# One core, sixteen attention bodies: TensorE's projections and scores moved ahead of the global queries' turn, and four of twelve key transfers handed to GpSimd

## What is computed

```python
def _layernorm(x, axis=-1, eps=1e-05): ...
mask = local(block of 64) | is_global[:, None] | is_global[None, :]   # 8 global tokens
q = split_heads(x @ Wq + bq)          # 16 heads of 8
k = split_heads(x @ Wk + bk)
v = split_heads(x @ Wv + bv)
scores = jnp.einsum('bhqd,bhkd->bhqk', q, k) / scale
scores = jnp.where(mask[None, None], scores, -jnp.inf)
attn = jax.nn.softmax(scores, axis=-1)
out = jnp.einsum('bhqk,bhkd->bhqd', attn, v)
return out.transpose(0, 2, 1, 3).reshape(B, S, E) @ Wo + bo
x = x + _L0_attn_ref(_layernorm(x, axis=-1), ...)
```

## Time and profile before

| | us |
|---|---|
| median of 3 runs | 567.05 (566.04 to 572.32) |
| profiled execution, its own time | 568.54 |
| its span, first to last instruction | 566.7 |

### The profile page before, as it was taken

The page is one execution under the profiler, slowest core; times in us unless marked ns, Lnnn a source line. Parts: engine busy times, 40 slices in busy tenths (PEclk is TensorE's granted clock), DMA queues, the critical chain, the costliest instruction groups (busy, mean ns, idle before and its releaser), DMA issues. The chain is left out here.

```text
span 566.7 us, 17496 instructions
## 1 busy us (share of the span) xinstructions
PE 469.9 (83%) x6139; PEld 348.1 (61%) x6139; DVE 409.6 (72%) x1247; ACT 296.8 (52%) x757; POOL 298.4 (53%) x588
## 2 busy tenths in 40 slices
PE   1977888888888888888999999999767999999810
PEld 1755666666666666545676676666544888888610
DVE  7566999999888888876889898987572434434337
ACT  2573665555556656524656656564424444444237
POOL 5543454444444334201358888777771577777720
PEclk9997999999999999969999999999989999999975
DMA  6626343455655655326233333332124334333158
GB/s 189 112 51 139 55 71 63 67 132 111 110 108 110 108 107 114 81 52 150 54 83 90 95 87 97 96 85 67 34 97 132 106 110 116 110 109 98 53 178 286
DMA packets 96006, 58.30 MB, mean 103 GB/s; under 512 B 24560, under 2 KB 92224, under 8 KB 95920
## 3 DMA queue, kind: packets, MB, share of 16 engines
q1 hardware_dynamic: 74448, 39.93, 30.2%
q10 hardware_dynamic: 16896, 7.34, 6.7%
q0 software_dynamic: 4576, 9.91, 5.1%
HBM read 20.76 MB, written 17.50 MB: 68 GB/s over the span
## 5 line engine op out<-in xcount | busy, mean ns | idle before, releaser
L507 POOL TENSOR_SCALAR veps<-mv 128x2 f32<-128x2 f32 x48 | 11.2, 232 | 144.9 <-issue 101.2
L1292 ACT ACTIVATE probs<-ps 128x512 f32<-128x512 f32 x128 | 73.3, 603 | 12.1 <-PE ps L1672 9.8
L613 POOL DMA_INDIRECT expert_in<-xn,sloti x64 | 65.5, 1023 | 17.6 <-issue 17.6
L1147 DVE TENSOR_TENSOR eh<-ps,sg 128x256 f32<-128x256 f32 x40 | 17.0, 425 | 59.8 <-ACT sg L1496 58.9
L772 DVE TENSOR_REDUCE nmax<-ps 128x8 f32<-128x512 f32 x64 | 42.5, 686 | 18.9 <-PE ps L1607 18.8
L666 POOL DMA_INDIRECT expert_out<-ey,xt x40 | 38.3, 957 | 27.0 <-DVE ey L1154 16.7
L772 DVE TENSOR_REDUCE mparts<-ps 128x8 bf16<-128x512 f32 x64 | 43.3, 687 | 6.7 <-PE ps L1662 6.3
L1607 PE MATMUL ps<-kbd,qs 96*64 96x128 bf16 x512 | 38.0, 293 | 4.5 <-DMA qs<-part 3.6
L2026 PE MATMUL ps<-wgu,turned 128*128 x160 | 41.3, 380 | 0.0
L1490 ACT COPY turned<-ps 128x512 f32<-128x512 f32 (+1 forms) x43 | 23.8, 554 | 28.5 <-PE ps L2019 23.2
L509 POOL TENSOR_TENSOR rstd<-veps,minus_half 128x2 f32<-128x2 f32 x48 | 35.8, 745 | 4.0
(11 more groups left out here) (248 smaller groups left out, 1360.2 us busy)
## 6 DMA issues: line engine op xcount, KB each, us to landing
kbd<-part SPq DMA_DIRECT2D x192, 32.0 KB
qs<-part ACTq DMA_DIRECT2D x93, 64.0 KB
xt<-expert_in SPq DMA_DIRECT2D x64, 72.0 KB
qs<-part SPq DMA_DIRECT2D x51, 64.0 KB
ck_scr<-wgu SPq DMA_DIRECT2D x6, 512.0 KB
ckbd<-ck_scr SPq DMA_DIRECT2D x16, 192.0 KB
kbd<-part SPq DMA_DIRECT2D x48, 64.0 KB
wgu<-in_L_ffn_gate_up_w SPq DMA_DIRECT2D x4, 512.0 KB, 4.0
```

The lines of the kernel that those rows point to most:

```text
L613: pool.indirect_dma_start(xs, bass.IndirectOffsetOnAxis(sloti[b % 3][:, n:n + 1], 0), xn3[b % 3][:, n // TOPK, n % TOPK, :], None).then_in ...
L1292: a_.activation(probs[:, 2 * i:2 * i + 2, :], P2[i % 2][:, :].rearrange("p (j q) -> p j q", j=2), ACT.Exp, scale=SCALE).then_inc(s("probs" ...
```

## The change

All of it holds for bodies 0 to 13 (`late(b)`); bodies 14 and 15 stay as they were.

- TensorE: behind `global_keys` now stand `self_project`, the first group of scores, and only then `global_query_turn`; the output product `self_out` moves from ahead of all these to behind the fourth group of scores. It now waits until ScalarE has read the projections out of bank A0, and `columns` waits until VectorE has taken the output product out of it.
- VectorE: `global_query_max` moves up behind the first transpose of `attended`; the first maxima stand ahead of the normalisation; `self_rest` moves from behind the second to behind the third maxima; `self_end` moves to the body's end.
- SyncE issues eight key transfers in place of twelve. GpSimd issues the other four (piece 4 of the second part, piece 2 of the third), ahead of its `rstd_of`. They have a semaphore of their own, `lent`; who waited for `got` now waits for both.

```diff
+        LENT = 4
+        GOT = {True: 16 * (3 * NP - LENT), False: 16 * NP}
+        def by_pool(b, i):
+            return i in (2, 4)
+        def late(b):
+            return 0 <= b < B - 2
...
-                        if K_PART[i] == k:
+                        if K_PART[i] == k and not by_pool(b, i):
...
+            def keys_regrouped(b, p):
+                at_least(pool, s_("gk_ps"), b - 1)
+                for i in (4, 2):
+                    pool.wait_ge(s_("part"), 3 * b + K_PART[i] + 1)
+                    for a in range(2):
+                        pool.dma_start(kbd[p][16 * i + 8 * a:16 * i + 8 * a + 8, :, a, :, :].rearrange("r j k n -> r j (k n)"),
+                                       part[64 * a:64 * a + 64, K_PART[i], S:2 * S]).then_inc(s_("lent"), 16)
...
                     self_global_heads(b + 1, 1 - p)
+                    keys_regrouped(b + 1, 1 - p)
...
                 v.transpose(turned_od, OD[:, :]).then_inc(s_("od_turned"), 1)
+                between()
...
-                    attended(b - 1)
-                if b == 0:
+                    attended(b - 1, lambda: global_query_max(b) if has(b) else None)
+                elif has(b):
                     self_last_part(1)
-                if has(b):
                     global_query_max(b)
...
-                if has(b - 1):
+                if has(b - 1) and not late(b):
                     self_end(b - 1)
...
+                if late(b):
+                    self_maxima(b + 1, 0, 0)
...
             def self_scores(b, p, u, half):
                 if u == 0:
                     pe.wait_ge(s_("got"), GOT[True] * b + GOT[True])
+                    pe.wait_ge(s_("lent"), 16 * LENT * (b + 1))
...
             def self_out(b):
                 pe.wait_ge(s_("att_all"), b + 1)
+                if late(b + 1):
+                    pe.wait_ge(s_("qk32"), 2 * (b + 3) + 2)
...
                     global_keys(b, p)
-                if has(b - 1):
-                    self_out(b - 1)
-                if has(b):
+                if late(b):
+                    self_project(b + 2)
+                    self_scores(b + 1, 1 - p, 0, 0)
                     global_query_turn(b)
-                if has(b + 2):
-                    self_project(b + 2)
...
+                    self_scores(b + 1, 1 - p, 0, 1)
                     self_global_values(b + 1)
-                    self_scores(b + 1, 1 - p, 0, 1)
+                    self_scores(b + 1, 1 - p, 1, 0)
                     global_query_out(b, p)
+                    self_scores(b + 1, 1 - p, 1, 1)
+                    if has(b - 1):
+                        self_out(b - 1)
```

More of the change, by code:

```diff
@@ L349, in decoder, with headed @@
         PLANNED = 14
-        GOT = {True: 16 * 3 * NP, False: 16 * NP}
+        LENT = 4
[4 more added lines that the diff above has]
+            return 0 <= b < B - 2
+        def headed(b):
+            return 3 * b + 2
         def sent_back(q):
@@ L550, in self_global_keys @@
                 pool.wait_ge(s_("got"), GOT[True] * b + GOT[True])
+                pool.wait_ge(s_("lent"), 16 * LENT * (b + 1))
                 at_least(pool, s_("gk_ps"), b)
@@ L554, in self_global_keys @@
                                          kbd[p][0:KROWS, :, :, :, :].rearrange("p j a k n -> p j a (k n)")[:, :, :, first:first + step * (n - 1) + 1:step])
-                last.then_inc(s_("kbg"), 1)
+                last.then_inc(s_("kgqg"), 1)
+            def keys_regrouped(b, p):
[5 more added lines that the diff above has]
+                                       part[64 * a:64 * a + 64, K_PART[i], S:2 * S]).then_inc(s_("lent"), 16)
             def lay_out_later_stages(b):
-                pool.wait_ge(s_("kgqg"), 2 * b + 4)
+                pool.wait_ge(s_("kgqg"), headed(b + 1))
                 for p in range(2):
@@ L597, in _ @@
             rstd_of(s_, 1)
+            keys_regrouped(0, 0)
             order(2, cwq)
@@ L783, in shift_spread, with attended @@
                     v.tensor_copy(qs[p][SHIFT:128, j::2, :], qs[p][SHIFT:128, 0:1, :].to_broadcast([32, PAIRS // 2 - j // 2, S])).then_inc(s_("mT"), 1)
-            def attended(b):
+            def attended(b, between):
                 turned_od = hT[:, :, :].rearrange("p t q -> p (t q)")
@@ L875, in self_body @@
                     global_rows(b - 1)
+                if has(b):
+                    global_query_sum(b)
                 if has(b + 3):
@@ L897, in self_body @@
                     cross_rest(1)
-                self_maxima(b + 1, 0, 0)
+                if not late(b):
+                    self_maxima(b + 1, 0, 0)
                 self_maxima(b + 1, 0, 1)
-                if has(b + 2):
+                if not late(b):
+                    if CROSS and b + 2 == B:
+                        cross_rest(0)
+                    if has(b):
+                        global_heads_out(b)
+                self_maxima(b + 1, 1, 0)
+                if late(b):
                     self_rest(b + 2, p)
-                elif CROSS and b + 2 == B:
-                    cross_rest(0)
-                if has(b):
                     global_heads_out(b)
-                self_maxima(b + 1, 1, 0)
                 self_maxima(b + 1, 1, 1)
@@ L910, in self_body @@
                     self_vg(b + 1, 1 - p)
-                    if has(b + 2):
+                    if late(b):
+                        if has(b - 1):
+                            self_end(b - 1)
                         self_last_part(b + 2)
@@ L1305, in cross_first_part @@
                     act.wait_ge(s_("got"), GOT[True] * B)
+                    act.wait_ge(s_("lent"), 16 * LENT * B)
                 at_least(act, c_("got"), GOT[False] * (b - 1))
@@ L1612, in self_global_scores @@
             def self_global_scores(b, p):
[L1613 removed]
+                pe.wait_ge(s_("kgqg"), headed(b))
                 at_least(pe, s_("probs"), 4 * (b - 1))
@@ L1695, in global_queries @@
             def global_queries(b, p):
-                pe.wait_ge(s_("kgqg"), 2 * b + 2)
+                pe.wait_ge(s_("kgqg"), headed(b))
                 at_least(pe, s_("gtmp"), b)
@@ L1701, in global_keys @@
                 pe.wait_ge(s_("probs"), 4 * b + 3)
-                pe.wait_ge(s_("kbg"), b + 1)
+                pe.wait_ge(s_("kgqg"), headed(b) + 1)
                 for odd in range(2):
@@ L1737, in self_body @@
                     self_global_scores(b + 1, 1 - p)
+                at_least(pe, s_("x_new"), b - 1)
                 if has(b + 2):
@@ L1756, in self_body @@
                     weigh(s_, b, p, 0, lambda n, j: vbd[p][:, n, j, :], NB)
-                if has(b - 1):
-                    if has(b + 2):
-                        pe.wait_ge(s_("xnT"), b + 3)
-                    elif CROSS and b + 2 < B + 2:
+                if has(b - 1) and not late(b):
+                    if CROSS and b + 2 < B + 2:
                         pe.wait_ge(c_("xnT"), b + 3 - B)
@@ L1771, in self_body @@
                     global_keys(b, p)
-                if has(b - 1):
-                    self_out(b - 1)
-                if has(b):
+                if late(b):
+                    self_project(b + 2)
+                    self_scores(b + 1, 1 - p, 0, 0)
                     global_query_turn(b)
-                if has(b + 2):
-                    self_project(b + 2)
-                elif CROSS and b + 2 < B + 2:
-                    pe.wait_ge(s_("x_new"), b)
-                    cross_project(b + 2 - B)
-                if has(b + 1):
-                    self_scores(b + 1, 1 - p, 0, 0)
+                    self_scores(b + 1, 1 - p, 0, 1)
                     self_global_values(b + 1)
-                    self_scores(b + 1, 1 - p, 0, 1)
-                if has(b):
+                    self_scores(b + 1, 1 - p, 1, 0)
                     global_query_out(b, p)
-                if has(b + 1):
-                    self_scores(b + 1, 1 - p, 1, 0)
                     self_scores(b + 1, 1 - p, 1, 1)
+                    if has(b - 1):
+                        self_out(b - 1)
+                else:
+                    if has(b - 1):
+                        self_out(b - 1)
+                    if has(b):
+                        global_query_turn(b)
+                    if CROSS and b + 2 < B + 2:
+                        pe.wait_ge(s_("x_new"), b)
+                        cross_project(b + 2 - B)
+                    if has(b + 1):
+                        self_scores(b + 1, 1 - p, 0, 0)
+                        self_global_values(b + 1)
+                        self_scores(b + 1, 1 - p, 0, 1)
+                    if has(b):
+                        global_query_out(b, p)
+                    if has(b + 1):
+                        self_scores(b + 1, 1 - p, 1, 0)
+                        self_scores(b + 1, 1 - p, 1, 1)
                 if CROSS and b + 1 == B:
```

8 lines of the change are left out of this document (3 added, 5 removed).

## The result

The changed kernel takes **593.08 us** (median of 6 runs, 588.72 to 595.83), the kernel before 569.23 us beside it (6 runs, 566.04 to 572.32): a ratio of 1.0421 with a 95% interval from 1.0374 to 1.0467. It is slower by 4.2%, and above the whole range forecast. The profiled execution took 595.83 us, its span is 594.0 us in place of 566.7.

A forecast was written before the change was run, and what follows sets the result against it. VectorE was taken to bound bodies 1 to 7, a new loop of 12.5 us bodies 8 to 13; gains of 2.2, 1.7 and 1.0 us (start), together 4.9, gave 562.2 us against the median, range 558 to 574.

The forecast's parts named there:

- The transfers: Key transfers: SyncE's eight landed after 8.6 us, GpSimd's four after 8.87 us, giving bodies 8 to 13 of 12.5 us.
- The new loop: Self-attention bodies: next key issues wait for this batch's first scores, 3.44 us from scores to issue, plus the keys' landing time.
- break-even of 9.4 us: Bodies 8 to 13: the longest the keys may take from first issue to landing without lengthening the 12.86 us body.
- Slow landing: Rival: GpSimd's last key transfer lands as late as SyncE's last does; body 14.0 us, 579.6 us in all; chance 0.15.
- Bodies 1 to 7: Self-attention bodies with extra work, taken as bound by VectorE: only one wait of 0.28 us each to gain, 1.7 us together.
- GpSimd's issue: GpSimd's four key transfers: 0.96 us each with 0.30 us ahead, taken from its indirect transfers.
- cheap bound: GpSimd's key transfers: issues as short as SyncE's, 0.67 us, so GpSimd's part is 6.5 us and VectorE's 12.12 us decides.
- cheap issues: Rival: GpSimd issues key transfers as cheaply as SyncE, bodies 8 to 13 fall to 12.12 us, 559.9 us; chance 0.24.
- VectorE shuts GpSimd out: Rival: VectorE's two `qs` copies each hold up a GpSimd issue by 0.42 us; loop 13.15 us, 568.4 us; chance 0.13.
- VectorE swallows it: Rival: VectorE waits for GpSimd's later power or for `part[1]`, leaving only the gain at the start; 566 us; chance 0.14.
- TensorE's and VectorE's order: Self-attention: TensorE's two waits go, scores start some 2.3 us earlier; VectorE's floor in bodies 8 to 13 falls to 12.12 us.
- The start: Body 0: SyncE's four dropped issues shorten TensorE's 3.56 us wait for the second batch's transfers, gaining 1.0 us (0 to 2).

The follow-up runs named there:

- e13: The changed kernel with each of SyncE's eight key transfers writing 16 partitions in place of 8 (keys in wrong places): 573.04 us, 1.010 of the kernel before.
- e1: The changed kernel with all twelve key transfers back on SyncE, the new order of TensorE and VectorE kept: 586.35 us, 1.035 of the kernel before.
- e14: The changed kernel with all twelve key transfers on SyncE, each over 16 partitions (keys in wrong places): 580.13 us, 1.022 of the kernel before.
- e10: The changed kernel with five extra products on TensorE ahead of the first scores, filling the wait for keys: 589.32 us, 1.041 of the kernel before.
- e11: The changed kernel with the global queries' turn back ahead of the first scores, plus four extra TensorE products before them: 577.45 us, 1.020 of the kernel before.
- e5: The changed kernel without GpSimd's four key transfers from the third batch on (old contents stay): 578.07 us, 1.016 of the kernel before.

## Why the prediction was wrong, point by point

**The step that failed is the landing in "The transfers"**, the term that set the body at 12.5 us. It had SyncE's eight landed 3.3 us behind the last issue's end, "as now", and GpSimd's last 2.23 us behind its issue: 8.6 and 8.87 us, G in all. Measured: the eight issues end after 5.35 us and the first scores start 5.6 us behind that; GpSimd's issues end after 168.88 + 2.49 - 165.77 = 5.60 us, and by then the scores are still 5.3 us off; G is 11.0 on the mean. The 3.3 us of the earlier trace rows were the tail of a queue that issues slowly enough for the engines nearly to keep up; with a third of the issues moved away the same bytes wait for the engines. The 2.23 us of the earlier trace rows were a transfer late in the kernel, with no queue but GpSimd's at work beside it; here its median is 4.2. With the keys over 16 partitions (e13) G is 9.2, close to the 8.9 I had. That is partly luck: GpSimd's four start later than I had it, issue faster and land later.

**The new loop was right**: 3.44 us of lag by the rows of before, 3.4 to 3.7 measured, and the break-even of 9.4 us for bodies 8 to 13 held (G 11.0 loses, e13's 9.2 breaks even). With G right the formula gives 14.4 us, against 14.48 and 14.73.

**Slow landing**, the rival with 0.15 of the chance, is what happened, at a larger size: 14.0 us and 579.6 us there. Its price was GpSimd's last transfer alone; it is SyncE's last too, 10.9 against 10.8 us behind the first issue. What I held against it, that SyncE and ScalarE have issued theirs when GpSimd's go out, is true and beside the point: issued is not moved. The Trainium skill has the rule for it (page "Trainium Kernel Development and Optimization", section "Key Constraints"): transfers issued from SyncE, ScalarE and GpSimd run on the same 16 engines, and issuing from several only saves issue time. e1 agrees with it: G is 10.8 with SyncE alone on the keys and 11.0 with GpSimd's help. Over 16 partitions the saved issue time does show: 10.2 (e14) and 9.2 (e13).

**Bodies 1 to 7** were taken as bound by VectorE, with a gain of 0.28 us each. With a loop of 12.5 us that followed, since 13.05 - 0.28 = 12.77 lies above it. At the measured G the loop is as long in both kinds of body, and costs 1.43 us in these.

**GpSimd's issue** was mis-sized, on the safe side: 0.63 us on the mean, in place of 0.96 and 0.30. I had called 0.67 the cheap bound; the case "cheap issues" held for the issue and did not matter, since the issue no longer set the landing.

**VectorE shuts GpSimd out** showed at the start, and hardly in the bodies. There four issues took 2.34 to 2.66 us, and one beside a `qs` copy 0.79 us at most; the least, median and most of all 64 are 561, 564 and 1351 ns. The longest two, 1.25 and 1.35 us, stand beside VectorE's casts at the start. GpSimd's and VectorE's timelines of the changed kernel:

```profile
16.70 4.01 POOL L579 DMA_DIRECT2D kbd<-part  x4 [0.25 <-ACT part L1303]
...
18.03 2.56 DVE L964 CAST kbd<-constants 32x2048 bf16<-32x2048 f32 x2
```

The rule that the prediction cites (the Trainium skill, page "SBUF — State Buffer", section "SBUF: two separate sides") has GpSimd shut out beside a copy in VectorE's fast mode. The casts agree with it in kind; a `qs` copy held up an issue by 0.2 us, not by its whole length of 0.42.

**VectorE swallows it** did not decide either; GpSimd kept its cover ahead of the power (4.82 us of idle time ahead of it).

**TensorE's and VectorE's order** did what the prediction said: the waits named there are gone. Early scores are no gain when their keys are not there.

**The start** was to give 1.0 us and costs 2.3. GpSimd's four stand in front of the first scores already. They landed at 28.1 us, SyncE's and ScalarE's at 25.5, and TensorE waits for them; TensorE's timeline of the changed kernel:

```profile
28.23 1.13 PE L1643 MATMUL ps<-kbd,qs 96*64 96x128 bf16 x16 [5.26 <-DMA kbd<-part]
```

where the kernel before starts them at 26.53. It goes with the hold beside the casts. In e10 and e13, which have the same four, only one issue was held up (1.17 and 1.19 us). There the four landed at 25.0 and 24.5, the first scores started at 26.43 and 26.47, and body 1 started 2.2 and 2.5 us earlier than before. In e13 (GpSimd's timeline):

```profile
16.72 3.17 POOL L579 DMA_DIRECT2D kbd<-part  x4 [0.25 <-ACT part L1303]
```

In the other eight kernels with the four, the changed one among them, they took 3.5 us or more and landed at 27.6 to 28.2. So the gain at the start was there to be had. That the hold takes it away is read from these ten executions; no run tests it by itself, and why the landing slips by 3 us where the issue slips by under 1 stays open.

**The clock** was not in the prediction. It costs nothing that shows in the closed loop (e10), and up to 0.9% in the open one (e11).

## What to carry to other kernels

When a consumer is moved ahead of the work that makes its next input, write down the body as lag plus G before anything else, and take G from a batch that moves all its bytes, not from the tail of a slow queue or from a lone transfer. If one queue issues at the pace at which the engines move, a second queue buys nothing; look first at how many engines a transfer's shape uses. A wait that is zero in one body and one or two microseconds in the next is the mark of lag plus G just over the body. Where the issue itself waits, all of the excess is lost; where it does not, half by calculation, and more in the runs here.

## What the runs showed of the hardware

A plain transfer of 32 KB issued by GpSimd took 0.63 us of its time on the mean, two thirds of an indirect one's 0.96 to 1.0, and 4.2 us (median) to land in this traffic. Beside VectorE's casts it took up to 1.35 us.

The first indirect transfer of GpSimd stood still longer where GpSimd had issued plain ones all through the self-attention. GpSimd's timeline, the kernel before:

```profile
289.51 1.22 POOL L613 DMA_INDIRECT expert_in<-xn,sloti  x1 [0.24 <-issue]
```

and the changed one:

```profile
316.49 1.14 POOL L640 DMA_INDIRECT expert_in<-xn,sloti  x1 [2.45 <-issue]
```

2.2 us, once. All nine kernels with 64 plain transfers have it (2.26 to 2.53 us of standing still), the seven without any do not (0.24 or 0.25 us), and neither does e5, with eight at the start (0.22 us). What GpSimd does in it no run here shows.

The 512-byte packets of SyncE's transfers took 74 ns on the mean when a transfer wrote 8 partitions and 35 ns when it wrote 16 (e13), with the same bytes. That half of the engines is full is worked out from events and packet times; the load of single engines was not read.
